# Wider scatter rows for a graph layer: groups of 1024 edges, ten slots and 26 buckets, with the scatters issued ahead of the gathers

## The reference

```python
# layer 0: sums over the neighbours, scaled by the degrees
norm = deg_inv_sqrt[row] * deg_inv_sqrt[col]
out = segment_sum(x[row] * norm[:, None], col)
x = layernorm(x + out)
# layer 1: src, dst = edge_index
gate = silu(edge_attr @ W1.T + b1) @ W2.T + b2 + sum(emb[z[src]] * (emb[z[dst]] @ adaptW.T))
cw = where(distances < 6, 0.5 * (cos(pi * distances / 6) + 1), 0)
mj = node_mult[dst]
msg = gate * x[dst] * (cw * mj)[:, None]
agg = segment_sum(msg, src) / clip(segment_sum(mj, src), 1e-8)
x = layernorm(x + layernorm_with_gamma_beta(x + agg))
```

## Time and profile before

| | us |
|---|---|
| median of 3 runs (3584.2 to 3595.98) | 3589.17 |
| the profiled execution | 3596.59 |
| its span | 3594.8 |
| main loop, first to last start of `messages` (100 tiles on) | 487.7 to 3191.6 |
| reduction, first to last instruction of the buckets | 3238.9 to 3502.6 |

### The profile page before, as it was taken

How to read it: one execution, slowest core, us unless ns; L and a number is a source line. 1 busy time by engine, 2 the same in 40 slices (tenths; PEclk the granted TensorE clock), 3 DMA queues, 4 the chain that set the end, 5 groups by cost and what they waited for, 6 DMA issues and landing times. The chain is left out here.

```text
span 3594.8 us, 69567 instructions
## 1 busy us (share of the span) xinstructions
PE 2457.2 (68%) x24398; PEld 2030.9 (56%) x24398; DVE 2434.8 (68%) x5609; ACT 1044.9 (29%) x2117; POOL 2265.9 (63%) x2116
## 2 busy tenths in 40 slices
PE   4899256677676767767677766767776767746760
PEld 3677145556555655656555655655555655646660
DVE  7755457777676776777776776777676777746654
ACT  0000123333333333333333333333333333421110
POOL 8700477777777777777777777777777777410002
PEclk9999987888788888888887877887887888868885
DMA  8000323333333333333333333333333333318871
GB/s 312 9 0 0 80 68 97 99 99 97 99 101 97 100 101 93 95 106 95 94 106 93 97 104 94 97 100 98 96 104 94 97 104 95 87 46 325 304 271 13
DMA packets 135012, 383.77 MB, mean 107 GB/s; under 512 B 53904, under 2 KB 53904, under 8 KB 128016
## 3 DMA queue, kind: packets, MB, share of 16 engines
q0 software_dynamic: 79200, 179.69, 18.7%
q1 hardware_dynamic: 53188, 198.17, 16.2%
q10 hardware_dynamic: 2284, 1.33, 0.1%
HBM read 258.83 MB, written 120.22 MB: 105 GB/s over the span
## 5 line engine op out<-in xcount | busy, mean ns | idle before, releaser
L630 POOL DMA_INDIRECT slot<-table,gidx x1616 | 1651.0, 1022 | 517.4 <-issue 485.0
L734 PEld LDWEIGHTS route<-parts,oh_r 128*128 128x128 bf16 x9696 | 810.1, 113 | 73.2 <-ACT routed L779 28.8
L734 PE MATMUL route<-parts,oh_r 128*128 128x148 bf16 x9696 | 828.8, 255 | 33.1 <-ACT routed L779 26.3
L779 ACT ACTIVATE routed<-route 128x444 bf16<-128x444 f32 x808 | 433.4, 541 | 770.4 <-PE route L734 763.7
L639 POOL DMA_INDIRECT perm<-routed,sidx x404 | 436.7, 1081 | 225.2 <-issue 207.1
L899 DVE TENSOR_SCALAR oh_r<-iota_r,spot 128x768 bf16<-128x768 f16 x1616 | 546.7, 413 | 5.2
L701 PE MATMUL rank<-oh_b,before 128*128 128x408 bf16 x202 | 87.7, 434 | 494.6 <-DVE oh_b L860 494.6
L870 DVE TENSOR_REDUCE spot<-rank 128x8 f32<-128x408 f32 x202 | 116.9, 579 | 407.9 <-PE rank L707 407.9
L701 PEld LDWEIGHTS rank<-oh_b,before 128*128 128x128 bf16 x202 | 20.2, 100 | 609.5 <-DVE oh_b L860 607.4
L668 PE MATMUL gate<-w,hid 97*128 97x96 f32 x1616 | 238.4, 294 | 161.2 <-DVE val L984 161.2
L828 ACT ACTIVATE parts<-val 128x392 bf16<-128x392 f32 x202 | 109.5, 542 | 746.3 <-DVE val L994 746.3
(11 more groups left out here) (209 smaller groups left out, 3502.7 us busy)
## 6 DMA issues: line engine op xcount, KB each, us to landing
rows<-perm SPq DMA_DIRECT2D x51, 1554.0 KB, 8.0
oh_t<-dst_row SPq DMA_DIRECT2D x101, 512.0 KB
attr<-in_edge_attr SPq DMA_DIRECT2D x101, 320.0 KB
slot<-table,gidx POOLq DMA_INDIRECT x1616
perm<-zeros SPq DMA_DIRECT2D x51, 444.0 KB, 13.6
perm<-routed,sidx POOLq DMA_INDIRECT x404
table<-tab SPq DMA_DIRECT2D x3, 676.0 KB, 4.7
xin<-in_x SPq DMA_DIRECT2D x1, 1224.0 KB, 9.8
```

The costliest lines, as they stand in the source:

```text
L630: e.indirect_dma_start(out=slot[:, s, g, :], out_offset=None, in_=table0, in_offset=bass.IndirectOffsetOnAxis(ap=gidx[:, s, g:g + 1], axis ...
L734: mm = e.matmul(route[:, bank, RC * j:RC * (j + 1)], oh_r[:, GR * g + q, bank * R // 2 + j, :], parts[:, s % 2, GR * g + q, :], start=(q = ...
L779: e.activation(routed[:, s % 2, g, bank * ROW // 2:(bank + 1) * ROW // 2], route[:, bank, 0:ROW // 2], ACT.Copy).then_inc(rows_ok, 1)
```

## The change

- Groups are 8 columns (1024 edges) instead of 4: 2 for each tile. Rows have R = 10 slots instead of 6. A bucket of the routing is 256 nodes: 26 instead of 51. `CAP` is 1024 rows, `CLEAR` 768 (256 for the last).
- `ranks` is called once for a tile, over 26 x 16 = 416 columns; its first two matmuls are one, and there are seven shifted ones. `routes` does 2 groups x 10 slots x 8 columns = 160 matmuls, in four phases of 3, 3, 2 and 2 slots over two banks (`PHASES`); ACT copies each phase.
- POOL's list is (scatter, 5), (gather, 0): the two scatters of the old tile stand ahead of the 16 gathers.
- The indices and the edge weights are stored to DRAM in the setup and loaded again tile by tile by SP; DVE's `indices` step is gone, and the third factor of the node (its multiplicity) is copied by ACT straight into `parts` instead of by DVE into `val`.
- The reduction loads 26 times 1024 rows, and works on each load twice, once for each half of the bucket: the one-hot has 10240 elements and there are 80 matmuls, 51 times.
- After the counting DVE makes two more tables (bucket and key of each edge), four operations over 1616 elements.

```diff
-GR = 4
+GR = 8
-R = 6
+R = 10
-CAP = 896
-CLEAR = 640
+CAP = 1024
+CLEAR = 768
+CLEAR_LAST = 256
+PHASES = ((0, 3), (3, 6), (6, 8), (8, 10))
...
+                    e.tensor_scalar(src_i[:, :], pid_i[:, :], 8, None, ALU.logical_shift_right).then_inc(mapped, 1)
+                    e.tensor_scalar(key_i, pid_i[:, :], 2 * P - 1, None, ALU.bitwise_and).then_inc(mapped, 1)
+                    e.tensor_copy(bkt16[:, :], src_i[:, :]).then_inc(mapped, 1)
+                    e.tensor_copy(key16[:, :], key_i).then_inc(mapped, 1)
...
+                    def edges(i, s):
+                        t = U * i + s
+                        cols = bass.ds(t * G, G)
+                        if since(i, s, U):
+                            e.wait_ge(gathered[s], 16 * G * i)
+                        e.dma_start(gidx[:, s, :], src_pid[:, cols]).then_inc(index_in[s], 16)
+                        if since(i, s, U):
+                            e.wait_ge(val_ok, 2 * (t - U + 1))
+                        e.dma_start(weight[:, s, :], weights[:, cols]).then_inc(weight_in[s], 16)
...
-                        over_tiles(e, NT, U, (load, 0), (rows, 0))
+                        over_tiles(e, NT, U, (edges, 0), (load, 3), (rows, 3))
...
-                        over_tiles(e, NT, U, (gather, 0), (scatter, 5))
+                        over_tiles(e, NT, U, (scatter, 5), (gather, 0))
...
+                            e.wait_ge(ohr, NG * t + g + 1)
+                            for phase, (a, b) in enumerate(PHASES):
+                                n = NPH * (NG * t + g) + phase
+                                if since(i, s, 1) or g or phase >= 2:
+                                    e.wait_ge(rows_ok, n - 1)
+                                for j in range(a, b):
+                                    for q in range(GR):
+                                        mm = e.matmul(route[:, phase % 2, RC * (j - a):RC * (j - a + 1)],
+                                                      oh_r[:, GR * g + q, j, :], parts[:, s % 2, GR * g + q, :],
+                                                      start=(q == 0), stop=(q == GR - 1))
+                                mm.then_inc(routing, 1)
...
-                        over_tiles(e, NT, U, (layer1(0), 3), (ranks(0), 3), (routes(0, 2), 4), (layer1(1), 3),
-                                   (rows_of_groups, 3), (ranks(1), 3), (routes(2, NG), 4), (pick(0), 3),
-                                   (layer2(0), 3), (pick(1), 3), (layer2(1), 3), (total, 0))
+                        over_tiles(e, NT, U, (layer1(0), 3), (ranks, 3), (routes(0), 4), (layer1(1), 3),
+                                   (rows_of_groups, 3), (routes(1), 4), (pick(0), 3), (layer2(0), 3), (pick(1), 3),
+                                   (layer2(1), 3), (total, 0))
...
                         for g in range(NG):
                             if since(i, s, 1):
-                                e.wait_ge(routing, 2 * (NG * (t - 1) + g + 1))
+                                e.wait_ge(routing, NPH * (NG * (t - 1) + g + 1))
...
-                            e.tensor_copy(val[:, m, :, C], got[:, m, :, TW - 1]).then_inc(val_ok, 1)
...
-                        for b in range(NP2):
-                            e.tensor_tensor(onehot[:, b % 2], count42[:, :, :], bc_mid(mine[:, b % 2], P),
-                            for c in range(AB * R):
+                        for h in range(NP2):
+                            e.tensor_tensor(onehot[:, h % 2], count[:, :, :], bc_mid(mine[:, h % 2], P),
+                            for c in range(COLS):
```

More of the change, by code:

```diff
@@ L37 @@
 ROW = R * RC
-CAP = 896
-CLEAR = 640
+CAP = 1024
+CLEAR = 768
+CLEAR_LAST = 256
 AB = CAP // P
-SPARE = NP2 * CAP
+SPARE = NB * CAP
 PERM = SPARE + NT * NG * P
@@ L232, in _ @@
                         e.dma_start(w2[2 * C:2 * C + 1, C * k:C * (k + 1)], b2).then_inc(wl, 16)
+                    e.wait_ge(mapped, 2)
+                    e.dma_start(src_pid, pid_i[:, :]).then_inc(stored, 16)
                     e.wait_ge(blank, 1)
-                    for b in range(NP2):
+                    for b in range(NB - 1):
                         e.dma_start(perm[CAP * b + CLEAR:CAP * (b + 1), :].rearrange("(p a) c -> p (a c)", p=P),
+                                    zeros[:, :]).then_inc(filled, 16)
+                    for k in range(FILLS_LAST):
+                        first = SPARE - (k + 1) * (CAP - CLEAR)
+                        e.dma_start(perm[first:first + CAP - CLEAR, :].rearrange("(p a) c -> p (a c)", p=P),
                                     zeros[:, :]).then_inc(filled, 16)
@@ L582, in build @@
             gathered = [sem(f"gathered{s}", ph) for s in range(U)]
+            index_in = [sem(f"index_in{s}", ph) for s in range(U)]
+            weight_in = [sem(f"weight_in{s}", ph) for s in range(U)]
             scattered = [sem(f"scattered{s}", ph) for s in range(2)]
@@ new lines, in ranks @@
+                    def ranks(i, s):
+                        t = U * i + s
+                        e.wait_ge(ohb, t + 1)
+                        if since(i, s, 1):
+                            e.wait_ge(placed, t)
+                            e.wait_ge(sx, t)
+                        at = rank[:, 0:NB * G].rearrange("p (b g q) -> p b g q", g=NG, q=GR)
+                        mine = oh_b[:, :, :].rearrange("p b (g q) -> p b g q", q=GR)
+                        e.matmul(at, lowered[:, :], mine, start=True, stop=False, skip_group_check=True)
+                        for k in range(1, GR):
+                            e.matmul(at[:, :, :, k:GR], ones16[:, :], mine[:, :, :, 0:GR - k], start=False,
+                                     stop=False, skip_group_check=True)
+                        e.matmul(at, ident_r[0:NT, bass.ds(t, 1)].broadcast_to([NT, P]),
+                                 rstart16[0:NT, :, :].unsqueeze(3).broadcast_to([NT, NB, NG, GR]),
+                                 start=False, stop=True, skip_group_check=True).then_inc(ranked, 1)
@@ L1222, in build @@
             RS = 3
[L1223 to L1226 removed]
+            COLS = AB * R
+            rows = sb("rows", [P, RS, COLS, RC], BF16, ph)
+            mine = sb("mine", [P, 2, COLS], BF16, ph)
+            count = sb("count", [P, P, COLS], BF16, ph)
+            onehot = sb("onehot", [P, 2, P, COLS], BF16, ph)
             three = sb("three", [P, 2, 3 * MW], F32, ph)
+            shift = sb("shift", [P, 2], F32, ph)
             acc = ps("acc", [P, 2, 512], F32, ph)
```

374 lines of the change are left out of this document (183 added, 191 removed).

## The result

The changed kernel takes 3871.73 us (3870.98 to 3872.89, 4 runs) and the kernel before, on the same chip, 3588.59 us: a ratio of 1.0787, 95% interval [1.0768, 1.0806]. The forecast was 4060 us, with a range from 3790 to 4240.

| stage | before | after | difference | forecast |
|---|---|---|---|---|
| until the first messages (setup, counting) | 487.7 | 495.5 | +8 | +9 |
| first to last start of the messages, 100 tiles | 2703.9 | 2893.5 | +190 | +410 |
| from there to the first load of the reduction | 40.7 | 40.7 | 0 | +3 |
| reduction, first load to last sum | 270.3 | 349.1 | +79 | +50 |
| last stage | 92.2 | 92.3 | 0 | 0 |

What follows compares the result with a forecast made beforehand. It took a ring of DVE and PE waiting for each other as the bound: loop +410, counting +7, setup +2, tail +3, reduction +50, together +472 on the profiled 3596.6, less 7.4: about 4060 us, range 3790 to 4240.

Steps and rivals of the forecast that it cites:

- the ring: Main loop: DVE and PE wait for each other in turn and set the tile; +4.1 us a tile, +410 us.
- Rival 3: Main loop: POOL was the bound after all, so two scatters less make the kernel faster, 3371 us; chance 0.04.
- The routes: Main loop, PE: all 160 route matmuls stand in the ring where 48 did, 12.9 us for 4.99, +7.9 a tile.
- The joints of the ring: Main loop: DVE's 4.95 us issue stand at the unrolled body's jump back, 0.8 a tile; PE's low-clock wait stays.
- The ranks: Main loop, PE: 2288 columns for 1836, 2.08 us for 1.67, +0.4 a tile.
- The odd tiles: Main loop, every second tile: DVE's window subtraction waits 2 us for ACT, 0.7 remain unhidden, 0.35 a tile.
- The hand-over: Main loop: 0.15 us stands against the second ranks and spot that go (1.09 + 0.81), -1.75 a tile.
- layer1 with rows_of_groups: Main loop, PE, between the route batches: 1.45 us; rows_of_groups has two groups for four, -0.5 a tile.
- one-hots and messages: Main loop, DVE: 8 one-hots in the ring for 16, 3.8 us for 5.38, -1.6; messages -0.45.
- Counting, setup, tail: Outside the steady loop: narrower counting matmuls +7 us, four more table operations in setup +2, tail of the loop +3.
- The reduction: Reduction stage: DVE's larger one-hots set 314 us for 264, +50, with the 80 matmuls hidden at 5.5 us.
- rival 1: Main loop: TensorE, being busier, runs all routes at the full clock, +202, 3791 us; chance 0.10.

Runs made afterwards that it cites:

- keeping the clock up: The changed kernel with 28 extra matmuls of 128 columns, results unread, ahead of TensorE's wait for the bucket one-hots: 3729.7 us, ratio 1.0385.

## Why the prediction was right, and where it was wrong

**What bounds the kernel**: right. GpSimd follows, the ring sets the tile. Moving layer1 (-113 us), keeping the clock up (-142 us with more work) and leaving out routes (-292 us) each pulled one link and moved the time; the order on GpSimd (+7 us) did not. Fewer scatters gave nothing, as forecast, though GpSimd saved less by them than I had counted: a scatter of the wider rows took 1504 ns for 1081, so 2.0 us a tile for 2.8. Rival 3 (faster, 3371) is out.

**The routes**: the step with the largest error, 1.5 us a tile too much, 11.4 for 12.9 when cut as in the forecast. All 160 are in the ring, as said. I had two prices: 69 ns at full rate from the second batch of the earlier trace rows, and 1.85 us for the low clock from the earlier trace rows.

The first was 3.31 us over 48 products. Those 3.31 us run to the end of the last product, and in them one weight load comes 193 ns and one 138 ns behind the load before, where nearly all others come at 63 to 68. From start to start a route costs 64.5 ns at the full clock, in the changed kernel's second batch: 10.3 us for 160, where I had 11.0.

The second held more than the clock. In a third of the tiles of the kernel before (32 of 93), PE stands behind the first 24 products of the second batch until ACT, which makes the window there, has copied a bank:

```profile
2090.56 1.72 PE L734 MATMUL route<-parts,oh_r 128*128 128x148 bf16 x24
2093.03 1.74 PE L734 MATMUL route<-parts,oh_r 128*128 128x148 bf16 x24 [0.74 <-ACT routed L779]
```

The weight loads are 1.02 us apart there, which is 0.3 us a tile in the mean. With 24 or 16 products to a bank instead of 12 this is gone. The low clock itself took 26 of the 96 products of a tile before, at some 60 ns more each 1.5 us, and 18 of 160 after, 1.1 us: I had kept its price, but the wait ahead of it was shorter now, 3.3 us for some 5.

**The joints of the ring**: 0.5 us too much, most of it at the jump back of the unrolled loop, where DVE stood 4.7 us in the mean before (65.9 us in 14 times) and 2.6 after (35.7 in 14); I had kept the 4.95 of one tile. The ranks were right, 2.05 for 2.08.

**The odd tiles**: 0.35 too much. The wait exists (154 us in the list), but ends before the second batch does, so it is hidden, and came out only when the ring around it was shortened.

**The hand-over** and layer1 with rows_of_groups: 0.2 us too little together, by the forecast's cuts (0.31 for 0.15, 1.50 for 1.45). With 0.15 too much on one-hots and messages, these terms make 31.3 - 29.0 = 2.3 us a tile, near the 2.2 by which the main term was too high.

**Counting, setup, tail**: +8 for +9, and 0 for +3. The 104 columns took 212 ns a product (171.5 / 808), for the 216 of the line through the earlier trace rows.

**The reduction**: +79 for +50. The step "the 80 matmuls take 5.5 us at full rate, hidden" failed. They take 6.4, since their weights lie 160 bytes apart, and with DVE's 5.8 below them PE became the bound. With blocks of 80 bytes DVE is the bound, 295 us, and the term comes to within 3 us of the forecast. This too low term hid 29 of the 220 us by which the loop's was too high, so the total looks better than its main term, of which less than half came.

**The range** held, since rival 1 (the full clock for all routes, 3791) was in it. The truth lay between it and the forecast: 18 of 160 routes at the low clock, and at a full-clock price below the one that rival 1 used.

## What to carry to other kernels

Where two engines wait for each other in turn, take every link as a mean over tiles, and price an instruction from start to start, with its pauses and its low clock counted apart; cut the links before and after at the same events; then look which order on which engine puts work into the ring that doesn't belong there. A link taken out gives its length until the next wait appears, which is mostly not the one you named: twice here it was an instruction ahead in the same engine's order. And if PE idles at a joint, products that nobody reads may be worth more than they cost.

## What the runs showed of the hardware

- TensorE's granted clock: behind a wait of some 3.3 us, 18 of the next 80 products (5 to 33) ran at 1.2 GHz, 121 to 125 ns each for 63 to 68. With 28 extra products ahead of the wait, 5 did. In the kernel before, behind some 5 us, 26 of 96 did.
- Products of 148 columns with weights side by side start 64.5 ns apart at the full clock, over 80 in a row. The Trainium skill (TensorE: Matmul & The Clock Gate, Part 2, Back-to-back issue gap) has about 81 ns for 128 columns in a sustained stream. These traces don't agree with it as it stands: 148 columns took less, and 147 columns took 80.0 ns only with weight columns 160 or 164 bytes apart.
- With weight columns 80 or 84 bytes apart a product of 147 columns takes 67 ns, with 160 or 164 it takes 80.
- On one chip the kernel before took a third longer (4753 us for 3591), and with GpSimd's order changed as long, with engines idle between their own instructions and single instructions as fast as elsewhere (a gather 1005 ns, for 1022). What held them up stays open.
